# Masked attention stages: a third head limited on VectorE in its own instruction, and penalties added on TensorE to one head in place of two

## What is computed

```python
attn = jnp.einsum('bnhd,bmhd->bhnm', q, k) * scale      # block 0: 8 x 16 heads x 512 x 512
attn = jnp.where(xa_mask[:, None, :, :], neg, attn)     # the same mask for all 16 heads
attn = jax.nn.softmax(attn, axis=-1)
out = jnp.einsum('bhnm,bmhd->bnhd', attn, v).reshape(B, N, C)
```

## Time and profile before

| | |
|---|---|
| median of 3 runs | 4929.38 us (4928.25 to 4931.38) |
| the profiled execution | 4919.61 us, of which the span in the trace is 4917.8 us |
| PE busy | 4589.4 us, 93% |
| DVE busy | 2994.1 us, 61% (7 to 8 tenths up to some 920 us and 6 to 7 tenths from some 1500 to 2300 us, less behind that) |
| ACT busy | 2304.8 us, 47% |
| POOL busy | 1062.8 us, 22% |
| penalties on PE, L706 | 512 weight loads, 2 in each of 256 steps |
| limits on DVE, L1200 | 256 of 128 x 1024, 323.2 us |

### The profile page before, as it was taken

The page is one execution under the profiler, slowest core; times in us unless marked ns, Lnnn a source line. Parts: engine busy times, 40 slices in busy tenths (PEclk is TensorE's granted clock), DMA queues, the critical chain, the costliest instruction groups (busy, mean ns, idle before and its releaser), DMA issues.

```text
span 4917.8 us, 66126 instructions
## 1 busy us (share of the span) xinstructions
PE 4589.4 (93%) x24369; PEld 1861.1 (38%) x24484; DVE 2994.1 (61%) x7970; ACT 2304.8 (47%) x3011; POOL 1062.8 (22%) x991
## 2 busy tenths in 40 slices
PE   6999999989998999999899989999989999999999
PEld 2333343433333333343444433343333333333334
DVE  6777776656668777676466675555524455454554
ACT  4455554466665444444455554444433334333333
POOL 0112221111111111111121111111113333333333
PEclk9999999999999999999999999999999999999999
DMA  1111111121121111011111211111110000000000
GB/s 61 35 50 56 51 42 43 35 91 55 61 67 52 37 39 34 31 35 49 66 62 62 74 63 47 38 35 49 40 65 22 13 1 13 13 13 13 1 13 9
DMA packets 164513, 201.67 MB, mean 41 GB/s; under 512 B 36321, under 2 KB 119649, under 8 KB 162914
## 3 DMA queue, kind: packets, MB, share of 16 engines
q1 hardware_dynamic: 141154, 176.34, 10.7%
q0 software_dynamic: 23040, 21.10, 1.7%
HBM read 128.86 MB, written 68.42 MB: 40 GB/s over the span
## 4 chain that ended last, share of the span: by engine, by line
PE 58%; issue 20%; DVE 13%; ACT 5%; DMA 2%; POOL 1%; SPq 0%; DVEq 0%; POOLq 0%; ACTq 0%
PE psO L725 7%; PE small L654 7%; PE small L661 6%; PE psT L700 5%; PE psT L930 5%; PE psS L682 4%; PE psT L783 3%; DVE nmb L1191 3%; ACT probs L1011 3%; PE psT L654 2%; PE psT L890 2%; PE psO L945 2%; PE psT L945 2%; PE psT L900 2%; DVE nmb L1188 2%
## 5 line engine op out<-in xcount | busy, mean ns | idle before, releaser
L1011 ACT ACTIVATE probs<-psT 128x1024 f32<-128x1024 f32 (+3 forms) x1280 | 1160.0, 961 | 1226.0 <-PE psT L700 1049.5
L1191 DVE TENSOR_REDUCE nmb<-psS 128x1 bf16<-128x512 f32 x1024 | 650.2, 684 | 347.5 <-PE psS L682 347.2
L1188 DVE CUSTOM_DVE_ANT_0 out<-psS,pens_sb 128x512 f32<-128x512 f32 x1024 | 666.2, 685 | 268.8 <-issue 267.5
L700 PE MATMUL psT<-low 32*128 32x512 f32 (+3 forms) x5120 | 735.1, 595 | 25.7 <-ACT probs L1011 22.8
L682 PE MATMUL psS<-out 32*128 32x512 bf16 (+3 forms) x2560 | 590.0, 374 | 111.3 <-DVE nmb L1188 50.0
L725 PE MATMUL psO<-probs,V 128*32 128x512 f32 (+3 forms) x5120 | 653.9, 583 | 9.2 <-DVE probs L1200 7.6
L1374 DVE TENSOR_REDUCE parts<-psS 128x2 bf16<-128x1024 f32 x256 | 314.9, 1230 | 531.3 <-PE psS L917 531.3
L1117 ACT ACTIVATE probs<-psT 128x1024 f32<-128x1024 f32 x256 | 262.2, 1024 | 524.9 <-PE psT L933 524.9
L682 PEld LDWEIGHTS psS<-out 32*128 32x128 bf16 x2560 | 149.5, 91 | 807.0 <-issue 440.7
L783 PE MATMUL psT<-out,W 128*128 128x512 f32 x768 | 382.9, 620 | 0.4
L1522 POOL TENSOR_TENSOR oN<-oN,probs 128x1024 f32<-128x1024 f32 x128 | 300.7, 2350 | 316.0 <-ACT probs L1117 315.6
(11 more groups left out here) (184 smaller groups left out, 5644.3 us busy)
## 6 DMA issues: line engine op xcount, KB each, us to landing
o_mid<-out SPq DMA_DIRECT2D x160, 256.0 KB, 2.0
oN<-o_mid POOLq DMA_DIRECT2D x160, 128.0 KB, 3.5
oN<-r_mid SPq DMA_DIRECT2D x80, 256.0 KB
x_mid<-xe SPq DMA_DIRECT2D x40, 512.0 KB, 2.9
xw<-x_mid SPq DMA_DIRECT2D x36, 512.0 KB, 4.1
xe<-x_mid SPq DMA_DIRECT2D x36, 512.0 KB, 5.0
cT<-ctxT SPq DMA_DIRECT2D x20, 512.0 KB, 5.1
W<-wm SPq DMA_DIRECT2D x6, 1024.0 KB, 8.3
```

The costliest lines, as they stand in the source:

```text
L700: last = nc.tensor.matmul(psT[j][:, q0:S], Kf[rows_of(j), q, a, c, kt * P:(kt + 1) * P], Qf[rows_of(j), q, a, c, q0:S], start=True, stop=p ...
L1011: nc.scalar.activation(probs[:, i % 2, two, q0:S], psT_all[:, two, q0:S], ACT.Exp, scale=float(DH) ** -0.5)\
L1188: nc.vector.tensor_tensor_reduce(junk[:, e, 0:n], psS[e][:, 0:n], penalty, 1.0, -3.0e38, ALU.add, ALU.max, at).then_inc(sem[f"s_read{e}"], 1)
L1191: nc.vector.tensor_reduce(at, psS[e][:, 0:n], AX, ALU.max).then_inc(sem[f"s_read{e}"], 1)
```

## The change

In the masked stages the penalty is added on PE to head 0 alone. Head 1 is limited on DVE by a new function, with an instruction of its own (128 x 512), since its exponential is done only with the second activation of the step. `limited` now counts two for each step, and `outputs` waits for both.

```diff
-        "pens": 3 if s == 0 else 0, "limited": STEPS if s in MASKED else 0,
+        "pens": 3 if s == 0 else 0, "limited": 2 * STEPS if s in MASKED else 0,
...
                 for j in (2, 3, 0, 1) if u.s in MASKED else range(4):
-                    plain = u.s != CAUSAL and not (u.s in MASKED and j < 2)
+                    plain = u.s != CAUSAL and not (u.s in MASKED and j == 0)
...
-                    if plain and j % 2:
+                    if plain and j % 2 and not (u.s in MASKED and j == 1):
                         last.then_inc(sem["st_full"], 1)
-                for j in range(2 if u.s in MASKED else 4 if u.s == CAUSAL else 0):
+                for j in range(1 if u.s in MASKED else 4 if u.s == CAUSAL else 0):
...
-                    if j % 2:
+                    if j % 2 or u.s in MASKED:
                         last.then_inc(sem["st_full"], 1)
...
                 if u.s in MASKED:
-                    pe.wait_ge(sem["limited"], count("limited", u, i + 1))
+                    pe.wait_ge(sem["limited"], count("limited", u, 2 * i + 2))
...
+            def limit_third(u, i):
+
+                dve.wait_ge(sem["exp_done"], count("exp_done", u, 2 * i + 2))
+                one = probs[:, i % 2, 1, :]
+                nc.vector.tensor_tensor(one, one, masking(lims, u)[:, i % T * S:(i % T + 1) * S], ALU.min).then_inc(sem["limited"], 1)
...
                 if cur is not None and cur.s in MASKED:
                     limit(cur, MLP_AFTER)
+                    limit_third(cur, MLP_AFTER)
...
                     between(place, 2 * i, prev, nxt)
+                    if of is not None and of.s in MASKED:
+                        limit_third(of, (i - 1) % STEPS)
                     for who, use in place.body.at(2 * i):
                         take(place, who, use, prev, cur, nxt)
```

## The result

| | before | after |
|---|---|---|
| median of 4 runs | 4928.82 us (4926.24 to 4931.38) | 5060.77 us (5058.67 to 5071.99) |
| ratio | | 1.0272, 95% interval 1.0255 to 1.029 |
| span of the profiled execution | 4917.8 us | 5056.9 us |
| mean granted clock of TensorE | 0.991 | 0.978 |

The account below looks back on a forecast made before the run. DVE's queue was taken to set the pace in steps 13 to 8 of the masked stages. 28.7 + 32.9 + 6 = 67.6 us on 4919.6 gave 4987.2, and 9.8 us for the median gave 4997.0 us; range 4946 to 5040 us.

Parts of the forecast that it names:

- What bounds the kernel: Masked stages, steps 13 to 8: DVE's queue sets the pace, with PE near its bound too; chance 0.62, 4997 us.
- Rivals 1, 2 and 4: 1: minimum hides, 4873 us, 0.12; 2: they cancel, 4929 to 4943 us, 0.13; 4: change does nothing, within 2.
- Rival 3: DVE sets the pace and keeps its idle time, +108 us, 5037 us; chance 0.13.
- The price of the parts: Each of 256 new minima takes 0.61 us of DVE's queue, 156 us in all; 256 weight loads go.
- The removed matmuls: Each is worth 0.22 us on PE; steps 9, 10 and 11 leave PE 0.66 us ahead at step 12.
- The layout of one body: Stage 0 body laid out again with one minimum more and one matmul less in each step: +4.1 us a body.
- The POOL term: Minima meeting POOL's multiplication wait at most about 1.1 us more in each of 15 bodies, 16 us.
- Stage 2: The same layout for bodies of stage 2, growing again in steps 7 and 8: +4.7 us a body.
- The first bodies: First bodies of the two masked stages, with room on DVE: +3 us each, between -3 and +10.
- The sum: Seven bodies at 4.1 us, seven at 4.7 and two first bodies at 3: 67.6 us more.

Follow-up runs that it names:

- the removal alone: The kernel before without head 1's 256 penalty matmuls in the masked stages and with no minimum added: 4944.4 us, ratio 1.0021.
- the filled kernel: The changed kernel with head 0's penalty added 4 times in steps 1, 2, 7 and 5 times in step 10 of MLP bodies: 5045.5 us, ratio 1.0224.
- the one aimed at that: The kernel before without head 1's penalty matmuls except in steps 11, 12 and 13, and with no minimum added: 4945.3 us, ratio 1.002.

## Why the prediction was wrong, step by step

Two things failed: the size of the delay, in the layout of one body and in the first bodies, and the clock, which the sum put at nothing. In the forecast's order:

- *What bounds the kernel.* Right. DVE's queue was full in steps 13 to 8, and a minimum there wasn't hidden. The sign and the main mechanism held. (PE is busy 91 to 97% in the windows of the earlier trace rows up to step 8, not 95 to 100%; nothing hangs on it.) Rivals 1, 2 and 4 didn't happen. Rival 3's time (5037 us) was nearer than the forecast's, and in stage 0 so was its reason, that DVE keeps its idle time. Steps 13 to 15, 0 to 3 and 4 to 8 of the undisturbed body of the kernel after:

```profile
504.28:517.45 13.17, 11.33 (x69) 3.95 (x71) 13.17 (x43) 5.82 (x6) 4.09 (x4) 1.00 0.54 169
404.90:423.51 18.61, 13.44 (x101) 5.37 (x99) 17.30 (x47) 12.61 (x12) 3.72 (x6) 1.00 0.22 63
423.51:449.30 25.79, 20.36 (x125) 8.54 (x127) 23.71 (x68) 16.22 (x19) 8.99 (x8) 1.00 0.05 20
```

  They take 57.6 us, where the forecast looked for 54 to 55, and DVE is busy for 54.2 of them (1.9 us of that is the minimum held up by POOL). That is 94%, not over 96%: 3.4 us stay idle, for 3.7 before.
- *The price of the parts.* Right: 0.60 us in DVE's queue for the forecast 0.61, and 256 weight loads left.
- *The removed matmuls.* The forecast gave PE 0.66 us a body in steps 9 to 11. Step 9 gave its 0.22 us, steps 10 and 11 gave nothing (5.56 and 4.33 us for 5.56 and 4.34), and step 12 gave 0.21. For step 10 the timeline of the kernel before has the reason, which the forecast passed over: PE waits there for DVE to take `small`, twice, whatever came ahead.

```profile
565.27 0.38 PE L766 MATMUL small<-identb,nmb 128*128 128x128 bf16 x4 [0.70 <-DVE xe L1263]
...
566.43 1.98 PE L654 MATMUL small<-hT,Wqkv 128*128 128x512 f32 x4 [0.78 <-DVE low L1224]
```

  For the whole kernel the removal alone brought nothing, since the clock takes back what undisturbed bodies gain.
- *The layout of one body.* This term was mis-sized: +4.1 us forecast, +6.8 us measured in the undisturbed body of stage 0. Up to the outputs of step 2 it was right within 0.2 us. Then it let the queue recover in steps 3 to 5, from 3.4 us late to 2.4; measured from the start of step 0 as above, PE is 4.5 us late at the end of step 5, where the forecast has 2.7. Of these 1.8 us, 1.4 are step 4 (6.06 us; 4.65 in bodies without POOL), where the minimum met POOL. Steps 6 to 8 added 2.1 us for the forecast's 1.5, steps 9 to 11 took off 0.2 for 0.4, and the rest is small change. The POOL term was put "in the range and not in the sum", at most 1.1 us a body; the minimum was held up by 1.9 us (2.58 us for 0.69). (The limit in the earlier trace rows ended 1.09 us behind POOL, not 1.14.) Without the meeting the body would be some 5.4 us longer than before.
- *Stage 2.* +4.7 us was forecast. The bodies with the least low clock (3.4 us) took 112.4 us for 104.9. Their fall is in step 8, which can be set beside step 8 of a body that kept its clock there:

```profile
1948.42:1952.62 4.20, 4.20 (x27) 1.34 (x23) 3.78 (x12) 2.82 (x4) 1.37 (x2) 1.00 0.01 2
2177.51:2183.36 5.85, 5.85 (x27) 1.77 (x23) 4.95 (x13) 2.82 (x4) 3.02 (x2) 0.71 0.00 0
```

  The fall costs 1.65 us there, so queue and wait make 5.8 us of the 7.5.
- *The first bodies.* +3 us each was forecast, at most +10. They took 104.5 and 98.3 us for 93.3 and 93.9, that is +11.2 and +4.4, with 27 and 13 us of low clock for 9.5 and 8.4.
- *The sum.* The seven bodies with an MLP took 62 us more in stage 0 (28.7 forecast) and 55 us more in stage 2 (32.9 forecast), the two first bodies 15.6 us more (6 forecast): 133 us for 67.6.
- *The clock.* This is the step that is missing altogether. The clock column of the earlier trace rows reads 1.00 in every window of a body with an MLP, and 0.95 and 0.96 in the first bodies, where PE waits most. The prediction read the ones, put the clock at nothing, and didn't ask what the delays of 0.6 to 3.9 us, which it forecast itself, would do to it. The price of a microsecond at the lower level was 0.29 us (bodies of the kernel after in stage 2: 2.0 us for 6.8), 0.38 (the removal alone) and 0.48 (step 8 above; the filled kernel). 122 us more at the lower level are then an estimate of 35 to 59 us. With that, 133 us in the two stages leave 74 to 98 us for queue and wait, for which 67.6 were forecast.
- *What stays open.* What the falls of the clock cost in the changed kernel was estimated from pairs of bodies and steps, not measured by a kernel without falls; the one aimed at that for the removal alone missed. Why the clock falls in one body and not in the next with the same work isn't shown either. That a kernel with more PE work is faster (5045.5 for 5060.8 us) shows the mechanism, not its full size.

## What to carry to other kernels

In this kernel two engines were both over 90% busy in the same stretch and handed work to each other in each step. Moving an instruction from one to the other cost half of its time in the receiver's queue (3.6 us a body for 12 x 0.60 us in the full steps) and, at the hand-over, a wait that was about as large again (3.0 to 4.4 us). Lay the queue out step by step, with what stands ahead of the new instruction, and then ask of each new wait on TensorE what the clock column will do: work taken off TensorE that only made it emptier brought nothing here. A change to the placement should also be tried where the receiver has room, but a gain of 0.1% was below what the wandering clock of this kernel lets one see.

## What the hardware showed that was not expected

- Taking 256 matmuls away, with nothing put in their place, gave 1.0021 (1.0003 to 1.0038), and adding 182 of them to the changed kernel saved about 15 us. Both go with the low clock in the masked stages (38 to 109 us, and 160 to 101 us).
- In stage 0 of the kernel with the matmul removed, bodies with the same instructions alternate between 104.5 us and 107.1 us, with none and 6.8 us of low clock: a body time measured once isn't the body's time, unless the clock stands beside it.
- A VectorE minimum of 128 x 512 with both operands in SBUF took 2.58 us where it met POOL's multiplication of 128 x 1024, for 0.69 us elsewhere.
